# First attention of a two-layer Flamingo-style block on one Trainium2 core: router logits from the turned input rows, eight more output columns, and the two scatters of a tile set apart

## The chip, the cores and the metric

The kernel runs on one core of a Trainium2 chip. The metric is the device time of one launch in microseconds (us), the median of several runs. Five engines work side by side, each through its own list of instructions in order: TensorE (PE, with its weight loads as PEld), VectorE (DVE), ScalarE (ACT), GpSimd (POOL), and the queue engine SyncE (SP), which here only issues transfers. They wait for each other through semaphores.

## The reference

32 sequences of 128 rows and 256 columns (x), each with a context of the same size, go through two layers. Layer 0 is what the change touches:

```python
x = x + tanh(g_xattn[0]) * L0_xattn(layernorm(x), ctx, ctx)       # 16 heads of 16
# L0_ffn of layernorm(x), a mixture of 8 experts, the best 2 of each row:
xn = (x - mu) / sqrt(var + eps) * gamma + beta
logits = xn @ Wg.T + bg                                           # 8 columns
tp, ti = top_k(softmax(logits), 2)
x = x + tanh(g_ffn[0]) * (layernorm(x) + sum of the two experts' outputs, weighted)
```

Here the layernorm in front of the mixture and the one inside it fall together in the kernel. Layer 1 (an attention with a bias per key, then a soft mixture over 16 slots) is left as it is.

## The kernel before

The program is a row of stages: setup, attention 0 with routing, the mixture of layer 0 (`moe0`), attention 1, the slot mixture, the final attention. Each stage of attention 0 is written as a loop over steps k from -2 to B+3 (B = 32 tiles, one sequence each), written out in full; in step k several tiles are in flight, each at another point. No planner sets the order: on each engine it is the order of the lines in `tensor`, `scalar`, `vector`, `gpsimd` and `sync`.

In step k of attention 0 TensorE does, in this order (line numbers of the profile):

- `scores(k, 0)`: half of the scores of tile k (L575) and of the turned scores of tile k-1 (L584, L590); L674 turns the output of tile k-2 back into rows
- `keys(k+1)` (L611) and `values(k+1)` (L598, three products of rounded parts)
- L687: the rank of each row of tile k-4 among the rows of its experts
- L704 turns the normalised rows `xh` of tile k+1; L720 turns the rows `xn` of tile k-3, normalised after the attention, into `ps[4]`
- `scores(k, 1)`: the other half; L728 turns the attention result `att` of tile k-2
- L750: the queries of tile k+1 from `xT`; L757: the 8 logits of tile k-3 from `xnT`; L764: the output product of tile k-2
- L789 turns the row maxima, L802 multiplies scores by values.

ScalarE empties what this fills. Its order in a step is: L900 (`avS`), the exponentials of the first half (L903), the keys (four L838) and values (L848) of tile k+1, `xT` (L924), `xnT` (L937), `aT` (L947), the exponentials of the second half (L951), the queries (two L963), `mT` (L968). It waits for the values before it begins with the keys, and `xT` comes behind both.

VectorE takes the maxima of each half (L1023, L1090), normalises rows (L1061 writes `xn`, L1112 writes `xh`), picks the best two logits (L1116 to L1122), counts rows per expert (L1065 to L1081 give the row numbers `slot_i`), adds the output product to x (L1132), and scales x by the gated layernorm (L1073, L1075, L1137). GpSimd computes the inverse roots (L1210; L1169 and L1171), adds the output bias (L1223), splits the context into two rounded parts (L1186, L1188), in steps 8 to 23 a sixteenth of the first expert's weights as well (L1241), and at the end of a step issues the two indirect DMAs (L1251, a GpSimd instruction of its own each) that scatter the rows `xn` of tile k-4 to their experts' regions.

Which two scatters and when:

```python
pool.wait_ge(st_p.sem, st_p.at(k - 1, "b"))     # TensorE has issued both halves of the turned scores
pool.wait_ge(rk_v.sem, rk_v.at(k - 4, "put"))   # slot_i of the tile is there
for c in range(2):
    nc.gpsimd.indirect_dma_start(...)
```

Of the kernel before, what the change touches and what calls it, by code (L numbers as in the profile page):

```python
# [7 lines left out]
ALU = mybir.AluOpType  # L8
ACT = mybir.ActivationFunctionType
# [36 lines left out]
COLS = ["bq0", "bk0", "bv0", "dbq", "dbk", "cbq", "cbk", "cbv", "gamma", "beta"]  # L46
# [15 lines left out]
def build(nc, a, out):  # L62
    ctx = ExitStack()
    with ctx:
# [93 lines left out]
        xnT = carve(C, P)  # L158
# [142 lines left out]
        assert 2 * C * D + 2 * C * P <= 4 * 2 * D  # L301
        ctx_hi, ctx_lo = (rounded(f"ctx_{part}", spare_at + (2 + n) * C * P, C, P) for n, part in enumerate(("hi", "lo")))
# [66 lines left out]
        ld_late = sem("ld_late")  # L369
# [26 lines left out]
        xn_columns = xn.rearrange("p i d -> p (i d)")[:, 0:4 * P].rearrange("p (n t) -> p n t", n=4)  # L396

        def folded(pe):
            pe.wait_ge(setup_v, 4)
            pe.wait_ge(ld_const, 16 * 5)  # L400
            for c in range(C):
                nc.tensor.matmul(ps[7][:, 0:D], xn_columns[:, c, :], w["o0"][:, c, :], start=c == 0, stop=c == C - 1)
# [5 lines left out]
        def tables(dve):  # L408
# [7 lines left out]
            for c in range(C):  # L416
                nc.vector.tensor_scalar(xn_columns[:, C + c, :], ones[:, :], col["beta"][:, c:c + 1], None, ALU.mult)
                last = nc.vector.tensor_scalar(xn_columns[:, c, :], ones[:, :], col["bv0"][:, c:c + 1], None, ALU.mult)
# [6 lines left out]
        def folded_rows(dve):  # L425
            dve.wait_ge(setup_p, 1)
            nc.vector.tensor_tensor(row["bo0"], ps[7][:, 0:D], row["bo0"], ALU.add).then_inc(setup_v, 1)
            nc.vector.tensor_tensor(bg_sb[:, :], ps[7][:, D:D + E0], bg_sb[:, :], ALU.add).then_inc(setup_v, 1)
            for c in range(C):
                nc.vector.tensor_scalar(wg_sb[:, c, :], wg_sb[:, c, :], col["gamma"][:, c:c + 1], None, ALU.mult)  # L430
# [5 lines left out]
        def attention(L):  # L436
# [6 lines left out]
            pre_p = track(n + "pre_p", "xT Q")  # L443
# [12 lines left out]
            out_v = track(n + "out_v", "den att x")  # L456
            ln_g = track(n + "ln_g", "var rstd")
            if A:
                rt_p = track(n + "rt_p", "xnT lg")
                rk_p = track(n + "rk_p", "rank")  # L460
                rk_v = track(n + "rk_v", "oh both pos run ohp slot put")
                rt_a = track(n + "rt_a", "xnT")
                rt_v = track(n + "rt_v", "lg top idx keep")
                bias_g = track(n + "bias_g", "x")
                n2_v = track(n + "n2_v", "stats mean rv xn grow shift res")
                n2_g = track(n + "n2_g", "rstd")
# [36 lines left out]
            def sync(sp):  # L503
                for k in steps:
                    if A and k == B - 1:
                        sp.wait_ge(kv_p.sem, kv_p.at(B - 1, "V"))
                        sp.wait_ge(pre_p.sem, pre_p.at(B - 1, "Q"))
# [40 lines left out]
            def tensor(pe):  # L548
# [93 lines left out]
                if A:  # L642
                    pe.wait_ge(ld_first, 32)
# [17 lines left out]
                for k in steps:  # L661
# [6 lines left out]
                    if A and k == 2:  # L668
                        pe.wait_ge(setup_v, 6)
# [1584 lines left out]
```

## Time and profile before

| | |
|---|---|
| runs | 1352.38, 1355.66, 1358.79 us; median 1355.66 |
| the profiled execution | 1369.84 us, span 1368.0 us, mean granted TensorE clock 0.981 |
| attention 0 | about 6 to 350 us of the span; first product of `moe0` at 359.68 us |
| TensorE busy (share of the span) | 1297.2 us (95%) |
| VectorE / ScalarE / GpSimd busy | 930.5 / 794.5 / 712.2 us |

A step of attention 0 takes 9.5 to 9.8 us; the steps 8 to 23, with the expert weights on ScalarE and GpSimd, are the longer ones. Matmuls in fp32 stand as two records for each instruction. "Idle before" an instruction names the engine that released it; "issue" is idle time for which the profile shows no cause.

### The profile page before, as it was taken

How to read it: one execution, taken by the hardware profiler on the slowest of the kernel's cores; microseconds unless marked ns; L12 is line 12 of the kernel's file. 1: busy time of each engine (PE TensorE's matmuls, PEld its weight loads, DVE VectorE, ACT ScalarE, POOL GpSimd, SP SyncE). 2: the span in 40 equal slices, each digit the busy share in tenths (PEclk: the TensorE clock that was granted, in tenths of full speed). 3: DMA queues.
4: the chain of work that ended last, by engine and by line, in shares of the span. 5: the costliest groups of instructions: out<-in, count | busy, mean ns of one | idle time of the engine just before them, and what ended most of it. 6: DMA issues, size and time to landing. Idle time of an engine off the chain costs nothing.

```text
span 1368.0 us, 38200 instructions
## 1 busy us (share of the span) xinstructions
PE 1297.2 (95%) x14802; PEld 1154.4 (84%) x14802; DVE 930.5 (68%) x2484; ACT 794.5 (58%) x1761; POOL 712.2 (52%) x708
## 2 busy tenths in 40 slices
PE   6999999998889999999999998999999999899898
PEld 5888888886789999999999986889999998545476
DVE  4788888897576655556556216999999997412287
ACT  4566666663457777777777444666566665332454
POOL 1365656553266877778877024566665652200131
PEclk9999999999899999999999997999999999999999
DMA  6574545463457777776775921541121110499812
GB/s 196 186 246 157 182 146 182 148 202 98 158 178 215 221 227 225 232 227 220 221 224 190 375 80 33 174 164 48 53 60 48 49 41 17 172 429 432 355 56 70
DMA packets 103618, 237.24 MB, mean 173 GB/s; under 512 B 8976, under 2 KB 85904, under 8 KB 91024
## 3 DMA queue, kind: packets, MB, share of 16 engines
q1 hardware_dynamic: 97296, 218.02, 46.3%
q0 software_dynamic: 6144, 16.79, 3.9%
q8 instruction: 119, 1.95, 0.6%
q14 instruction: 59, 0.48, 0.1%
HBM read 173.96 MB, written 60.82 MB: 172 GB/s over the span
## 4 chain that ended last, share of the span: by engine, by line
PE 85%; DVE 8%; DMA 3%; issue 2%; ACT 2%; POOL 0%; SPq 0%; DVEq 0%; ACTq 0%; PEldq 0%; POOLq 0%
PE ps L1542 13%; PE psT L1527 7%; PE ps L598 5%; PE psS L575 5%; PE ps L802 5%; PE ps L750 4%; PE psT L584 4%; PE psS L1527 3%; PE ps L1527 3%; PE ps L611 3%; PE ps L735 2%; PE ps L764 2%; PE ps L674 2%; PE psT L590 2%; PE ps L1780 2%
## 5 line engine op out<-in xcount | busy, mean ns | idle before, releaser
L1495 POOL TENSOR_TENSOR wb_lo<-arena,wb_hi 128x2048 fp32r<-128x2048 f32 x64 | 298.0, 4657 | 104.4 <-ACT wb_hi L1615 104.4
L1542 PE MATMUL ps<-wb_hi,hT_hi 128*128 128x256 f32 x528 | 153.3, 290 | 6.5 <-DVE hT_lo L1668 6.5
L584 PE MATMUL psT<-arena 32*128 32x128 f32 x2048 | 155.3, 286 | 0.0
L1542 PE MATMUL ps<-wb_lo,hT_hi 128*128 128x256 f32 x528 | 148.6, 281 | 0.0
L1542 PE MATMUL ps<-wb_hi,hT_lo 128*128 128x256 f32 x528 | 148.6, 281 | 0.0
L575 PE MATMUL psS<-arena 32*128 32x256 f32 x1024 | 143.2, 397 | 0.7 <-ACT arena L963 0.7
L1615 ACT CAST wb_hi<-arena 128x1024 fp32r<-128x1024 f32 x128 | 130.6, 1044 | 6.5 <-DMA arena<-w_dram 6.2
L1169 POOL TENSOR_TENSOR arena<-arena,eps_sb 128x1 f32<-128x1 f32 x96 | 26.2, 273 | 203.2 <-DVE arena L1043 115.4
L584 PEld LDWEIGHTS psT<-arena 32*128 32x128 f32 x2048 | 129.2, 188 | 2.6 <-issue 1.8
L1680 DVE TENSOR_TENSOR arena<-ps,arena 128x512 f32<-128x512 f32 (+1 forms) x39 | 25.4, 650 | 120.1 <-PE ps L1542 79.7
L1542 PEld LDWEIGHTS ps<-wb_hi,hT_hi 128*128 128x128 f32 x528 | 100.3, 190 | 6.8 <-issue 6.7
L575 PEld LDWEIGHTS psS<-arena 32*128 32x128 f32 x1024 | 93.6, 189 | 13.6 <-issue 11.5
L1542 PEld LDWEIGHTS ps<-wb_lo,hT_hi 128*128 128x128 f32 x528 | 101.5, 192 | 0.0
L1177 POOL DMA_INDIRECT arena<-xs_rows,slot_i x64 | 64.3, 1005 | 69.3 <-DMA xs_rows<-arena 54.3
L1542 PEld LDWEIGHTS ps<-wb_hi,hT_lo 128*128 128x128 f32 x528 | 100.3, 190 | 0.0
L1090 DVE TENSOR_REDUCE arena<-psS 128x8 f32<-128x1024 f32 x64 | 78.1, 1220 | 24.3 <-PE psS L575 24.3
L1023 DVE TENSOR_REDUCE arena<-psS 128x8 f32<-128x1024 f32 x64 | 78.3, 1224 | 20.0 <-PE psS L575 18.7
L1630 ACT ACTIVATE psS<-psS,arena 128x256 f32<-128x256 f32 x66 | 26.8, 444 | 99.8 <-PE psS L1527 99.8
L1251 POOL DMA_INDIRECT xs_rows<-arena,slot_i x64 | 65.3, 1020 | 35.9 <-issue 15.5
L838 ACT ACTIVATE arena<-ps,bkm,const 128x128 f32<-128x128 f32 x128 | 48.1, 456 | 46.5 <-PE ps L598 34.4
L750 PE MATMUL ps<-arena,w_sb 128*128 128x128 f32 x512 | 71.0, 283 | 2.8 <-ACT arena L924 2.8
L802 PE MATMUL ps<-arena 128*32 128x128 f32 x2048 | 70.0, 277 | 0.2
(385 smaller groups left out, 3894.4 us busy)
## 6 DMA issues: line engine op xcount, KB each, us to landing
arena<-wset_dram SPq DMA_DIRECT2D x24, 2048.0 KB, 15.5
xs_rows<-arena SPq DMA_DIRECT2D x33, 1024.0 KB, 8.2
arena<-w_dram SPq DMA_DIRECT2D x32, 1028.0 KB, 6.0
arena<-w_dram SPq DMA_DIRECT2D x32, 1024.0 KB, 5.9
arena<-w_dram SPq DMA_DIRECT2D x7, 2052.0 KB, 12.9
w_sb<-xs_rows SPq DMA_DIRECT2D x33, 256.0 KB, 2.7
xs_rows<-arena SPq DMA_DIRECT2D x33, 256.0 KB, 5.5
arena<-ctxT_dram SPq DMA_DIRECT2D x63, 128.0 KB, 2.4
```

What stands on the lines that cost most here:

```text
L575: last = nc.tensor.matmul(psS[:, b, c * D:(c + 1) * D], qT[p, k % 3, c, :], kbd[p, k % 3, c, :, :], start=A, stop=A or c == 1, skip_group_ ...
L584: nc.tensor.matmul(psT[:, b, j * P:(j + 1) * P], kbd[p, (k - 1) % 3, c, par, :], qT[p, (k - 1) % 3, c, :], start=j == 0, stop=False, skip_ ...
L598: last = nc.tensor.matmul(out_, left[i_][:, c, :], right[j_][:, c, :], start=n_ == 0 and c == 0, stop=n_ == 2 and c == C - 1)
L750: last = nc.tensor.matmul(ps[6][:, m * P:(m + 1) * P], wq[:, c, m * P:(m + 1) * P], xT[:, c, :], start=c == 0, stop=c == C - 1)
L802: last = nc.tensor.matmul(ps[4][32 * j:32 * (j + 1), g * P:(g + 1) * P], vz[:, (k - 1) % 3, 4 * g + j, :, :], pT[:, g, j * P:(j + 1) * P], ...
L1023: nc.vector.tensor_reduce(mx[:, 0:2, :], psS.rearrange("p b (j t) -> p b j t", j=4), AX, ALU.max, negate=True).then_inc(mx_v.sem, 1)
L1090: nc.vector.tensor_reduce(mx[:, 2:4, :], psS.rearrange("p b (j t) -> p b j t", j=4), AX, ALU.max, negate=True).then_inc(mx_v.sem, 1)
L1251: nc.gpsimd.indirect_dma_start(out=xs_dram[:, :], out_offset=bass.IndirectOffsetOnAxis(ap=slot_i[:, c, k - 4:k - 3].bitcast(U32), axis=0), ...
L1495: nc.gpsimd.tensor_tensor(wb_lo[:, u % 2, part], wb_raw[:, u % 2, part], wb_hi[:, u % 2, part], ALU.subtract).then_inc(w_g.sem, 1)
L1527: last = nc.tensor.matmul(ps[1 + f // 2][:, o:o + 2 * P], wp[:, c, f * P:(f + 1) * P], xp[:, c, :], start=n == 0 and c == 0, stop=n == 2 a ...
L1542: last = nc.tensor.matmul(ps[5][:, t * D:(t + 1) * D], hp[:, f, t * P:(t + 1) * P], wp[:, f, :], start=f == 0 and t == 0 and n == 0, stop= ...
L1615: last = nc.scalar.copy(wb_hi[:, b, o:o + F0], wb_raw[:, b, o:o + F0])
```

## The change

The logits no longer need the rows after the attention turned on TensorE. With x the input rows, a the attention's output before its output matrix Wo, t = tanh(g), and W the router's columns times gamma with their mean taken out, the sum (x + t (a Wo + bo) ) W is x W + t a (Wo W) + t bo W, and the layernorm's factor is applied to it afterwards. So:

- `wc` (W) is made in the setup by VectorE, with a product of ones on TensorE for the mean (`gate_sums`); Wo W takes four small products with a turned copy of Wo that is loaded in addition (`gate_through_output`) and stands behind Wo as 8 more columns of `wo_wide`; the bias row takes four more (`gate_biases`).
- TensorE: L720 is gone; the logits' product takes `xT` of tile k+1 and `wc`, right behind the queries; the output product has 264 columns for 256.
- ScalarE: `xnT` (L937) is gone; in its place it scales x by the gated layernorm (before VectorE's L1137); behind `mT` comes a small activation that undoes the input's normalisation on the 8 logit columns (`u`).
- VectorE: L1073, L1075 and L1137 are gone; one small operation comes in (`lg_sum`).
- GpSimd: four small operations come in (`spread`, `grow`, `shift`, `u`); the bias is added a step later; the second scatter of a tile is issued a step later, behind the first half of the scores, and the first one before the context parts.

The diff, cut to its core:

```diff
+        def gate_sums(pe):
+            pe.wait_ge(fold_v, 1)
+            for c in range(C):
+                last = nc.tensor.matmul(ps[4][:, 0:E0], ones[:, :], wc[:, c, :], start=c == 0, stop=c == C - 1)
...
+        def gate_through_output(pe):
+            pe.wait_ge(fold_v, 3)
+            for m in range(C):
+                for c in range(C):
+                    last = nc.tensor.matmul(ps[7][:, D + (1 + m) * E0:D + (2 + m) * E0], wo_turned[:, c, m * P:(m + 1) * P],
+                                            wc[:, c, :], start=c == 0, stop=c == C - 1)
...
+        def gate_biases(pe):
+            pe.wait_ge(fold_v, 4)
+            pe.wait_ge(setup_v, 6)
...
                 if A:
-                    pe.wait_ge(ld_first, 32)
+                    gate_sums(pe)
+                    pe.wait_ge(ld_first, 48)
                     pe.wait_ge(ld_kv, 16)
...
-                    if A and valid(k - 3):
-                        pe.wait_ge(n2_v.sem, n2_v.at(k - 3, "xn"))
...
-                        for c in range(C):
-                            last = nc.tensor.transpose(ps[4][:, c * P:(c + 1) * P], xn[:, (k - 3) % 3, c * P:(c + 1) * P],
-                                                       cv["ident"])
...
-                    if A and valid(k - 3):
-                        pe.wait_ge(rt_a.sem, rt_a.at(k - 3, "xnT"))
+                    if A and valid(k + 1):
...
-                            last = nc.tensor.matmul(ps[5][:, D:D + E0], xnT[:, c, :], wg_sb[:, c, :],
-                                                    start=c == 0, stop=c == C - 1)
+                            last = nc.tensor.matmul(ps[5][:, D:D + E0], xT[:, c, :], wc[:, c, :], start=c == 0, stop=c == C - 1)
...
-                                last = nc.tensor.matmul(ps[7][:, D:2 * D], aT[:, c, :], wo[:, c, :],
+                                last = nc.tensor.matmul(ps[7][:, 0:D + E0], aT[:, c, :], wo_wide[:, c, :],
...
                     if A and valid(k - 3):
-                        act.wait_ge(rt_p.sem, rt_p.at(k - 3, "xnT"))
-                        nc.scalar.copy(xnT.rearrange("p c t -> p (c t)"), ps[4][:, 0:D]).then_inc(rt_a.sem, 1)
+                        act.wait_ge(n2_g.sem, n2_g.at(k - 3, "shift"))
+                        act.wait_ge(n2_v.sem, n2_v.at(k - 3, "xn"))
+                        nc.scalar.activation(x_all[:, k - 2], x_all[:, k - 2], ACT.Identity, bias=rs[:, 1:2], scale=rs[:, 0:1])\
+                            .then_inc(n2_a.sem, 1)
...
-                    if A and valid(ln_i):
-                        dve.wait_ge(n2_v.sem, n2_v.at(ln_i, "shift"))
-                        nc.vector.tensor_scalar(x_all[:, ln_i + 1], x_all[:, ln_i + 1], rs[:, 0:1], rs[:, 1:2],
-                                                ALU.mult, ALU.subtract).then_inc(n2_v.sem, 1)
...
+                    if A and valid(k - 5):
+                        if valid(k - 1):
+                            pool.wait_ge(st_p.sem, st_p.at(k - 1, "a"))
+                        scatter(k - 5, 1)
```

**TensorE, a whole step between the values of tile k+1 and the maxima.** Before, from the row of values on (the numbers are lines of the kernel before):

```order
L598 MATMUL ps<-v_hi,ctx_lo 128x256 x2
L687 MATMUL ps<-both_r,before_r 128x8
L687 MATMUL ps<-both_r,both_rows 128x8
L704 MATMUL ps<-const,arena 128x128 x2
L720 MATMUL ps<-const,arena 128x128 x2
L575 MATMUL psS<-arena 128x256 x2
```

The rows from the second half's end on, before:

```order
L728 MATMUL ps<-const,arena 128x128 x2
L750 MATMUL ps<-arena,w_sb 128x128 x4
L757 MATMUL ps<-wg_sb,arena 128x8 x2
L764 MATMUL ps<-w_sb,arena 128x256 x2
L789 MATMUL ps<-ident_b,m_49 128x128
```

The same two places with the change (L648 is the old L598, L740 the old L687, L757 the old L704, L625 the old L575, L795 the old L750, L802 the logits, L808 the output):

```order
L648 MATMUL ps<-v_hi,ctx_lo 128x256 x2
L740 MATMUL ps<-both_r,before_r 128x8
L740 MATMUL ps<-both_r,both_rows 128x8
L757 MATMUL ps<-const,arena 128x128 x2
L625 MATMUL psS<-arena 128x256 x2
```

```order
L773 MATMUL ps<-const,arena 128x128 x2
L795 MATMUL ps<-arena,w_sb 128x128 x4
L802 MATMUL ps<-arena 128x8 x2
L808 MATMUL ps<-arena 128x264 x2
L833 MATMUL ps<-ident_b,m_49 128x128
```

Two instructions (L720) are gone between the values and the queries; behind the queries the count is the same.

**GpSimd, one step with a piece of the expert weights.** Before, from the row of the inverse roots on:

```order
L1210 TENSOR_TENSOR arena<-arena,mhalf 128x2 [waits a0_n2_v]
L1169 TENSOR_TENSOR arena<-arena,eps_sb 128x1 [waits a0_ln_v]
L1171 TENSOR_TENSOR arena<-arena,mhalf 128x1 [waits a0_ln_g]
L1223 TENSOR_TENSOR x_all<-x_all,row_sb 128x256 [waits a0_ln_v]
L1186 TENSOR_SCALAR ctx_hi<-arena 128x256 [waits a0_kv_p,a0_ld_ctx1]
L1188 TENSOR_TENSOR ctx_lo<-arena,ctx_hi 128x256 [waits rest_g]
L1241 TENSOR_TENSOR wb_lo<-arena,wb_hi 128x256 [waits first_hi]
L1251 DMA xs_rows<-arena,slot_i 33792x256 [waits a0_rk_v,a0_st_p,zeroed1]
L1251 DMA xs_rows<-arena,slot_i 33792x256
```

With the change (L1261 is a scatter, L1292 and L1293 are `grow` and `shift`, L1234 is `spread`, L1311 is `u`):

```order
L1284 TENSOR_TENSOR arena<-arena,mhalf 128x2 [waits a0_n2_g,a0_rt_v,a0_n2_v]
L1261 DMA xs_rows<-arena,slot_i 33792x256 [waits a0_st_p]
L1292 TENSOR_SCALAR arena<-arena,tg 128x1 [waits a0_n2_a,a0_n2_g]
L1293 TENSOR_SCALAR arena<-arena 128x1
L1228 TENSOR_TENSOR arena<-arena,eps_sb 128x1 [waits a0_ln_g,a0_ln_v]
L1230 TENSOR_TENSOR arena<-arena,mhalf 128x1 [waits a0_ln_g]
L1234 TENSOR_TENSOR arena<-arena 128x1 [waits a0_u_a,a0_ln_g]
L1307 TENSOR_TENSOR x_all<-x_all,row_sb 128x256 [waits a0_ln_v]
L1311 TENSOR_TENSOR arena<-arena 128x8 [waits a0_u_a]
L1261 DMA xs_rows<-arena,slot_i 33792x256 [waits a0_rk_v,a0_st_p,zeroed1]
L1250 TENSOR_SCALAR ctx_hi<-arena 128x256 [waits a0_kv_p,a0_ld_ctx1]
L1252 TENSOR_TENSOR ctx_lo<-arena,ctx_hi 128x256 [waits rest_g]
```

One scatter now stands second in the step, ahead of `grow` and `shift`, which ScalarE waits for; the other stands ahead of the context parts.

## Rows read from the trace of the kernel before

**Rows 1.** windows, 103:260: length, busy PE, PEld, DVE, ACT, POOL

```profile
103.00:260.00 157.00, 154.91 (x2248) 135.06 (x2247) 137.76 (x501) 100.81 (x239) 96.15 (x143) 1.00 0.49 165
```

**Rows 2.** waits of the weight loads, 58:316, then twice 316:349: us, times, longest

```profile
PEld ps L720 <- DVE arena L1061: 5.6, 15, 0.4
...
PEld ps L720 <- DVE arena L1061: 4.7, 4, 1.6
...
PEld ps L757 <- ACT arena L937: 1.2, 2, 0.7
```

**Rows 3.** timeline, step 19: start, us, engine, line

```profile
203.48 0.48 PE L598 MATMUL ps<-v_hi,ctx_hi 128*128 128x256 f32 x2
...
204.47 1.50 ACT L838 ACTIVATE arena<-ps,bkm,const 128x128 f32<-128x128 f32 x4 [1.17 <-PE ps L598]
...
204.94 0.20 PEld L720 LDWEIGHTS ps<-const,arena 128*128 128x128 f32 x2 [0.33 <-DVE arena L1061]
...
205.31 0.19 PEld L575 LDWEIGHTS psS<-arena 32*128 32x128 f32 x2 [0.17 <-issue]
...
206.11 0.40 ACT L924 COPY arena<-ps 128x256 f32<-128x256 f32 x1
...
206.92 1.06 PE L750 MATMUL ps<-arena,w_sb 128*128 128x128 f32 x8
```

**Rows 4.** timeline, step 26

```profile
271.32 0.48 PE L598 MATMUL ps<-v_hi,ctx_hi 128*128 128x256 f32 x2
...
273.95 0.41 ACT L924 COPY arena<-ps 128x256 f32<-128x256 f32 x1
...
274.82 1.06 PE L750 MATMUL ps<-arena,w_sb 128*128 128x128 f32 x8
...
278.22 0.48 PE L575 MATMUL psS<-arena 32*128 32x256 f32 x2
```

**Rows 5.** timeline, step 2 (no L720, no L687)

```profile
34.91 0.47 PE L598 MATMUL ps<-v_hi,ctx_hi 128*128 128x256 f32 x2
...
37.53 0.40 ACT L924 COPY arena<-ps 128x256 f32<-128x256 f32 x1
...
37.99 1.16 PE L750 MATMUL ps<-arena,w_sb 128*128 128x128 f32 x8 [0.21 <-ACT arena L924]
```

**Rows 6.** groups by line, 60 to 316 us: busy us, mean ns, idle before

```profile
L1090 DVE TENSOR_REDUCE arena<-psS 128x8 f32<-128x1024 f32 x27 | 33.1, 1225 | 14.6 <-PE psS L575 14.6
...
L1112 DVE TENSOR_SCALAR arena<-x_all,arena 128x256 f32<-128x256 f32 x26 | 13.0, 501 | 0.0
...
L1137 DVE TENSOR_SCALAR x_all<-x_all,arena 128x256 f32<-128x256 f32 x27 | 11.2, 413 | 0.0
...
L1251 POOL DMA_INDIRECT xs_rows<-arena,slot_i x54 | 55.4, 1026 | 18.0 <-issue 14.0 <-PE psT L590 4.0
...
L1169 POOL TENSOR_TENSOR arena<-arena,eps_sb 128x1 f32<-128x1 f32 x25 | 7.0, 281 | 43.4 <-DVE arena L1057 43.4
```

**Rows 7.** timeline, PE, step 3

```profile
43.74 0.48 PE L598 MATMUL ps<-v_hi,ctx_hi 128*128 128x256 f32 x2
...
46.45 0.44 PE L720 MATMUL ps<-const,arena 128*128 128x128 f32 x2 [1.52 <-DVE arena L1061]
...
48.62 1.92 PE L750 MATMUL ps<-arena,w_sb 128*128 128x128 f32 x8
...
55.00 0.48 PE L575 MATMUL psS<-arena 32*128 32x256 f32 x2
```

**Rows 8.** windows, 48 to 50 us; 0.53 is the granted clock

```profile
48.00:50.00 2.00, 2.00 (x17) 1.90 (x12) 1.86 (x6) 1.14 (x2) 0.84 (x2) 0.53 1.06 369
```

**Rows 9.** timeline of TensorE, setup

```profile
6.44 2.07 PE L611 MATMUL ps<-arena,w_sb 128*128 128x128 f32 x8 [6.44 <-DMA col_sb<-cols_dram]
...
22.86 0.51 PE L404 MATMUL ps<-wg_sb,arena 128*128 128x8 f32 x4
```

**Rows 10.** timeline of TensorE, last rank matmul of stage one

```profile
348.13 0.54 PE L687 MATMUL ps<-both_r,before_r 128*128 128x8 f32 x1
```

More of the change, by code:

```diff
@@ L157, in build @@
         xn = carve(3, D)
-        xnT = carve(C, P)
+        small_at = place[0]
+        wc = carve(C, E0)
+        lg_x = carve(4, E0)
+        lg_row = carve(E0)
+        lg_sum = carve(E0)
+        spread = carve(4)
+        ntg = carve(1)
+        carve(C * P - (place[0] - small_at))
         xc = carve(D)
@@ L666, in tensor @@
                         queries(pe, 0, 6)
+                    if A and k == 2:
+                        gate_biases(pe)
                     scores(k, 0)
                     if A and k == 2:
-                        pe.wait_ge(setup_v, 6)
+                        pe.wait_ge(fold_v, 5)
                     if valid(k - 2):
@@ L795, in tensor @@
                         if A:
-                            before(pe, rt_a.sem, rt_a.at(k - 3, "xnT"))
                             before(pe, rk_v.sem, rk_v.at(k - 4, "run") if valid(k - 4) else 0)
@@ L807, in tensor @@
                         folded(pe)
+                        gate_through_output(pe)
                     if A and k == B + 2:
@@ L968, in scalar @@
                         nc.scalar.copy(mT[:, :], ps[6][:, 0:P]).then_inc(m_a.sem, 1)
+                    if A and valid(k + 1):
+                        act.wait_ge(pre_p.sem, pre_p.at(k + 1, "x"))
+                        act.wait_ge(ln_g.sem, ln_g.at(k + 1, "spread"))
+                        before(act, out_v.sem, out_v.at(k - 3, "t"))
+                        nc.scalar.activation(lg_x[:, (k + 1) % 4, :], ps[5][:, D:D + E0], ACT.Identity, bias=0.0,
+                                             scale=spread[:, (k + 1) % 4:(k + 1) % 4 + 1]).then_inc(u_a.sem, 1)
                     if not A and valid(k - 4):
@@ L1007, in vector @@
                         dve.wait_ge(n2_v.sem, n2_v.at(ln_i, "stats"))
+                        before(dve, n2_g.sem, n2_g.at(ln_i - 1, "shift"))
                         nc.vector.bn_aggr(mv[:, 1, :], stat[:, 1, :]).then_inc(n2_v.sem, 1)
@@ L2148, in vector @@
                                         cv["parity"][:, None, :].to_broadcast([P, C, 2]), ALU.mult).then_inc(setup_v, 1)
+                for c in range(C):
+                    last = nc.vector.tensor_scalar(wc[:, c, :], wg_sb[:, c, :], col["gamma"][:, c:c + 1], None, ALU.mult)
+                last.then_inc(fold_v, 1)
             return sync, None, None, vector, None
```

174 lines of the change are left out of this document (116 added, 58 removed).

## The prediction

> **What bounds the kernel now.** I read the windows view first. In the long middle of attention 0, TensorE is busy for 154.91 of 157 us, VectorE for 137.76, ScalarE for 100.81, GpSimd for 96.15 [rows 1]. A step there takes some 9.7 us, so TensorE's list in order is the bound, VectorE is next with 8.5 us a step, and the other two have 3 us to spare. Then I asked what TensorE's weight loads wait for: between 58 and 316 us only L720, for VectorE's `xn`, 5.6 us in total [rows 2]. So L720 costs its wait and its own slot. The reader should see that the time of one step is a closed walk through TensorE's list, and that one piece of this walk has a second limit beside it. In step 19 the first product of the values starts at 203.48, the queries (L750) at 206.92: 3.44 us. In this stretch ScalarE waits for the values (L838, idle 1.17 us until TensorE's L598), does the keys, the value copy and `xT` (L924, from 206.11 for 0.40 us, to 206.51), and only then may L750 start [rows 3]. In step 26 the same is 271.32 to 274.82, 3.50 us, with L924 done at 274.36 [rows 4].
>
> **Steady steps.** The change takes L720 out of this stretch and adds nothing to it. On TensorE alone this is the wait of 0.33 and the load of 0.20, after which L575 would come at 204.78 where it is at 205.31: 0.53 us earlier [rows 3]. But ScalarE's chain starts at the values and doesn't move. Step 2 shows the stretch without L720 (and without L687): values at 34.91, L924 done at 37.93, L750 at 37.99 after waiting for L924; 3.08 us, of which 0.06 lies between L924's end and L750 [rows 5]. So L750 can't come before 206.51 + 0.06 = 206.57 in step 19 (gain 0.35) and 274.42 in step 26 (gain 0.40). The other 0.13 to 0.18 us become a new wait, of L750 for ScalarE. From L750 on, TensorE's list is as long as before: the logits' product only moves ahead of other data, and the output has 8 more columns in 256, which by L404's size (4 records of 8 columns, 0.51 us, [rows 9]) is bounded by 0 and some 0.25; I take 0.03, since the output's own time is by columns. In steps 4 to 30 queries and L720 both occur: 16 with the expert weights, 16 x 0.32 = 5.1 us; 11 without, 11 x 0.37 = 4.1. Together **-9.2 us**; bounds: 0, if another engine takes the place of L720's wait, and 27 x 0.53 = 14.3.
>
> What hides the rest. VectorE loses L1137 (413 ns on average) and two of about 0.2 to 0.3, and gains one of some 0.15 on 8 columns. In its second half it still sits idle 14.6 us over 27 steps before L1090, 0.54 each [rows 6]; the scores come 0.53 earlier and VectorE is ready earlier by the two small ones, so some 0.2 to 0.3 us of that idle time stay. The scaling of x moves to ScalarE in the place of a copy of the same size, and a small one comes behind `mT`; ScalarE has 3 us a step. Behind the waiting scaling stand `aT`, the second exponentials and the queries' copies, and for them L764 and L802; so `shift` must not be late. GpSimd needs for it L1210's result, one scatter (1026 ns and some 0.26 of issue gap) and two operations of 281 ns [rows 6]: about 2.6 us after L1210 starts, where ScalarE comes to it some 4.7 us after (L924's end at 206.51 [rows 3]). GpSimd's whole step grows from 96.15/157 of 9.7 = 5.9 us busy by 4 x 0.28 = 1.1 to 7.1, plus issue gaps. The transfers themselves are 2 scatters of a tile as before, through the same queue; `xn`'s buffer is used again three tiles later, so a scatter issued a step later still has a step to land.
>
> The Trainium skill speaks against this place for a scatter. L1112 and the same operation elsewhere differ by what runs beside them: L1112, beside the scatters, takes 501 ns, L1137 takes 413 [rows 6]. The Trainium skill, SBUF — State Buffer, section "SBUF: two separate sides", says that VectorE in some modes and GpSimd lock each other out of one shared pair of ports for a whole instruction. By the row this is 0.1 us on one operation; by that rule a scatter could hold one VectorE operation for its whole 1.0 us, in a part of the step where VectorE has only some 0.25 us of idle time left, which is the second rival.
>
> **Step 3.** Here L720 waits 1.52 us, the queries come 4.88 us after the values (43.74 to 48.62), and TensorE then runs at half its clock (granted 0.53 [rows 8], so 1.2 GHz for most of it): L750 takes 1.92 us instead of 1.06, and from L750 to the next step's L575 at 55.00 are 6.38 us, against 3.40 in step 26 [rows 4, 7]. With ScalarE's chain as the limit the queries come at 43.74 + 3.08 = 46.8: **-1.8**. If TensorE then keeps 2.4 GHz, another 6.38 - 3.40 = **-3.0**. The idle stretch of 1.52 us stands just before the fall, and shrinks to a few tenths; but whether the fall hangs on it no row shows. I take it as the likelier, bounds 0 and 3.0.
>
> **Setup.** TensorE's first product waits for a load (6.44 [rows 9]) and then runs without a break. Now `gate_sums` comes first: it waits for one more load in the list and VectorE's two scalings of it, and is two products of 8 columns: 0.5 by L404, plus some 0.9 for the wait, between 0.5 and 2: **+1.4**. `gate_through_output` and `gate_biases` are four such products each, on TensorE's path: **+1.8**. The logits' product begins four steps earlier; in steps -1 to 1 it lies in a wait for the queries' copy, in step 2 it doesn't: **+0.4**. On GpSimd the first bias, which waited for the setup, moves out of the way of the first context parts: -0.1. Sum **+3.5** (2 to 6).
>
> **The end of the stage.** In steps 31 to 34 there are no keys, so L720's waits are bare: 4.7 us in 4 times, and L757 waits 1.2 for `xnT` [rows 2]. Those 5.9, four loads of 0.2 and four logits' products of 0.5 make 8.7 us that leave TensorE's list; the lower bound is 0. VectorE's and ScalarE's chains give part back: in step 31, the second maxima can come only 1.2 earlier, and steps 32 and 33 are bound by exponentials and `aT`, so little comes there. The last rank matmul (348.13 [rows 10]) stands behind the ahead-of-time products of attention 1 in TensorE's list, and two waits and four instructions leave the list just before it. I take **-3.6**, from 1.2 in step 31, 0.7 by step 33, 1.7 in step 34, nearer the lower end. The routing and `moe0`'s first product come behind it by the same amount.
>
> **Sum.** -9.2 - 1.8 - 3.0 + 3.5 - 3.6 = -14.1 us. The profiled execution, 1369.84 us (span 1368.0 and 1.8 around it), would become 1355.7. It lies 14.2 above the median of the runs shown, 1355.66; taken off this median the forecast is **1341.5 us**. Without the clock's 3.0 it is 1344.5.
>
> **Rivals.** (1) *Only the setup and the tail change.* Another chain closes the steady step at its old length: VectorE, whose remaining idle time the fuller GpSimd beside it eats up. Then -1.8 + 3.5 - 3.6 = -1.9, or with the clock -4.9: 1351 to 1354. For it: GpSimd is fuller, and L1112 shows that the two touch each other. Against: L1090's idle time is real now, and three VectorE operations leave. Chance 0.14. (2) *Slower: `shift` comes too late.* GpSimd's scatter stands ahead of `grow` and `shift`, ScalarE waits for them with `aT` and the exponentials behind it. It decides if the scatter, measured at 1.0, takes over 1.0 + 2.1 = 3.1 us; each microsecond beyond costs 27 to 32 us. At 4 us this is 0.8 x 30 = 24 - 4.9 = +19: 1375. The rule of the ports would be its cause. Against: 54 scatters average 1026 ns, though VectorE works through all of them. Chance 0.07. (3) *The forecast without the clock*, or with other falls of it instead: part of the forecast's own range. (4) *More than forecast*, the tail at its upper bound, 8.7: 1336.
>
> **How the numbers follow.** Forecast with its variants (3) and (4): 0.79. A measurement of this kernel tells about 0.5% (6.8 us) from no change. Faster by more, below 1348.9: 0.78; within: 0.14; slower: 0.08. The range takes in the upper bound of the tail and the lower edge of rival 1: 1334 to 1352.
>
> **What would show it.** L750 must wait for ScalarE's L924 in nearly every step, 0.1 to 0.2 us, and the steps must take 9.1 us without and 9.4 with the expert weights. L808 (the output) must not wait for `aT`. Step 3 must take some 9.7 us at full clock instead of 13.9. TensorE's first keys should start at about 7.8 us. The last rank matmul should come some 14 us earlier than 348.13. Wrong would be: L750 without a wait, ScalarE waiting for GpSimd's `shift`, or L1090 without idle time in front of it.

## The result

The changed kernel took 1349.53 us (median of 20 runs, 1341.31 to 1357.38), the kernel before 1363.57 beside it (20 runs, 1351.39 to 1368.82). The estimate of the ratio from all runs is 0.9925, 95% interval 0.9903 to 0.9947: 0.75%, or 10.2 us, faster. The means of the runs lie 11.1 us apart (1350.43 and 1361.55) and the medians 14.0; this text goes by the estimate that has an interval. A second series of 12 runs (after_again) gives 0.9915 (0.9883 to 0.9947). The profiled execution took 1357.0 us with a span of 1355.2, against 1369.84 and 1368.0 before.

The windows of the changed kernel over the middle of attention 0 answer to [rows 1]:

```profile
core 0: us, PE busy (x) PEld busy (x) DVE busy (x) ACT busy (x) POOL busy (x), PEclk, DMA share, GB/s
103.00:260.00 157.00, 156.19 (x2321) 135.32 (x2321) 145.86 (x491) 110.02 (x270) 120.56 (x220) 1.00 0.53 176
```

VectorE is fuller (145.86 of 157 where it was 137.76), although work left it. The waits of TensorE's weight loads from 58 to 307 us answer to [rows 2] (us in total, times, longest):

```profile
PEld psS L625 <- issue: 9.7, 53, 0.2
PEld ps L795 <- ACT arena L972: 7.0, 27, 0.3
PEld ps L833 <- issue: 4.5, 25, 0.2
PEld ps L845 <- issue: 1.5, 7, 0.3
PEld ps L648 <- POOL ctx_lo L1252: 0.8, 1, 0.8
```

The reader is to see that L720's wait is gone and that the queries (L795, before L750) wait for ScalarE's `xT` (L972, before L924) in each of 27 steps, 0.26 us each. In the timeline of a step, answering to [rows 3], TensorE's and ScalarE's rows that matter are:

```profile
209.87 0.48 PE L648 MATMUL ps<-v_hi,ctx_hi 128*128 128x256 f32 x2
210.87 1.50 ACT L882 ACTIVATE arena<-ps,bkm,const 128x128 f32<-128x128 f32 x4 [1.18 <-PE ps L648]
212.26 0.38 ACT L892 COPY arena<-ps 128x256 f32<-128x256 f32 x1
212.51 0.40 ACT L972 COPY arena<-ps 128x256 f32<-128x256 f32 x1
212.77 0.64 ACT L986 ACTIVATE x_all<-x_all,arena 128x256 f32<-128x256 f32 x1
212.96 0.97 PEld L795 LDWEIGHTS ps<-arena,w_sb 128*128 128x128 f32 x8 [0.26 <-ACT arena L972]
212.96 1.16 PE L795 MATMUL ps<-arena,w_sb 128*128 128x128 f32 x8
213.28 0.40 ACT L997 COPY arena<-ps 128x256 f32<-128x256 f32 x1
213.53 1.07 ACT L1001 ACTIVATE arena<-psT 128x1024 f32<-128x1024 f32 x1
214.32 1.14 PE L808 MATMUL ps<-arena 128*128 128x264 f32 x4
214.44 0.67 ACT L1013 ACTIVATE arena<-ps,qcol 128x128 f32<-128x128 f32 x2
215.30 0.22 PE L833 MATMUL ps<-ident_b,m 128*128 128x128 bf16 x1
```

Values to queries are 3.09 us (209.87 to 212.96); the step is 9.26 to 9.27 long in most cases. Between the first products of the values in step 2 and in step 30 lie 260.95 us, 259.90 in the second profile; before they were 274.58, and 271.02 in a second profile of the old kernel.

The early part costs more than it did, and runs partly at half clock (1.2 GHz):

```profile
10.00:20.00 10.00, 8.39 (x58) 6.57 (x57) 6.41 (x24) 4.91 (x15) 1.55 (x5) 1.00 0.73 254
20.00:30.00 10.00, 9.54 (x64) 8.82 (x63) 2.42 (x6) 2.89 (x8) 0.54 (x2) 0.54 0.27 93
30.00:40.00 10.00, 8.96 (x124) 7.64 (x124) 3.91 (x13) 4.60 (x12) 2.75 (x5) 0.84 0.40 134
```

Step 2's values start at 41.90, 7.0 later than in the old profile [rows 5], which has half clock itself from 14.0 to 17.4 us.

### The profile page after: what moved, and what is told of

Read it like the earlier page. It is cut to its first block, busy times and chain, and to the rows that moved or that the text cites. A ratio compares the mean times of both kernels' runs of the same rounds, so it can differ in the third digit from the quotient of the medians.

```text
span 1355.2 us, 38313 instructions
## 1 busy us (share of the span) xinstructions
PE 1287.3 (95%) x14758; PEld 1145.5 (85%) x14758; DVE 932.6 (69%) x2426; ACT 805.6 (59%) x1794; POOL 748.0 (55%) x836
## 4 chain that ended last, share of the span: by engine, by line
PE 83%; DVE 6%; DMA 4%; issue 2%; ACT 2%; POOL 1%; SPq 1%; DVEq 0%; ACTq 0%; POOLq 0%; PEldq 0%
PE ps L1632 12%; PE psT L1617 6%; PE ps L648 6%; PE psS L625 5%; PE ps L795 5%; PE ps L845 5%; PE psT L634 4%; PE ps L661 4%; PE ps L1617 3%; PE psS L1617 3%; PE ps L780 2%; PE ps L727 2%; PE ps L808 2%; PE psT L640 2%; DMA arena<-w_dram 2%
## 5 line engine op out<-in xcount | busy, mean ns | idle before, releaser
L634 PE MATMUL psT<-arena 32*128 32x128 f32 x2048 | 151.9, 287 | 0.4 <-ACT arena L948 0.4
L625 PE MATMUL psS<-arena 32*128 32x256 f32 x1024 | 143.5, 399 | 1.2 <-ACT arena L948 0.5
L1705 ACT CAST wb_hi<-arena 128x1024 fp32r<-128x1024 f32 x128 | 130.6, 1045 | 13.4 <-DMA arena<-w_dram 13.2
L625 PEld LDWEIGHTS psS<-arena 32*128 32x128 f32 x1024 | 95.4, 191 | 13.6 <-issue 10.6
L1147 DVE TENSOR_REDUCE arena<-psS 128x8 f32<-128x1024 f32 x64 | 78.0, 1219 | 11.1 <-PE psS L625 10.8
L1261 POOL DMA_INDIRECT xs_rows<-arena,slot_i x64 | 68.7, 1073 | 19.7 <-issue 11.5
L795 PE MATMUL ps<-arena,w_sb 128*128 128x128 f32 x512 | 72.8, 286 | 3.1 <-ACT arena L972 2.6
L795 PEld LDWEIGHTS ps<-arena,w_sb 128*128 128x128 f32 x512 | 63.4, 195 | 12.0 <-ACT arena L972 10.8
## 6 DMA issues: line engine op xcount, KB each, us to landing
arena<-wset_dram SPq DMA_DIRECT2D x24, 2048.0 KB, 14.6
arena<-w_dram SPq DMA_DIRECT2D x7, 2052.0 KB, 13.6
```

What stands on the lines that cost most here:

```text
L625: last = nc.tensor.matmul(psS[:, b, c * D:(c + 1) * D], qT[p, k % 3, c, :], kbd[p, k % 3, c, :, :], start=A, stop=A or c == 1, skip_group_ ...
L634: nc.tensor.matmul(psT[:, b, j * P:(j + 1) * P], kbd[p, (k - 1) % 3, c, par, :], qT[p, (k - 1) % 3, c, :], start=j == 0, stop=False, skip_ ...
L795: last = nc.tensor.matmul(ps[6][:, m * P:(m + 1) * P], wq[:, c, m * P:(m + 1) * P], xT[:, c, :], start=c == 0, stop=c == C - 1)
L1147: nc.vector.tensor_reduce(mx[:, 2:4, :], psS.rearrange("p b (j t) -> p b j t", j=4), AX, ALU.max, negate=True).then_inc(mx_v.sem, 1)
L1261: nc.gpsimd.indirect_dma_start(out=xs_dram[:, :], out_offset=bass.IndirectOffsetOnAxis(ap=slot_i[:, c, i:i + 1].bitcast(U32), axis=0), in_ ...
L1705: last = nc.scalar.copy(wb_hi[:, b, o:o + F0], wb_raw[:, b, o:o + F0])
```

## The experiments

"Step" below is the time between the first products of the values of two tiles (L598 or L648), median of the profile; "ring steps" are the 16 with the expert weights. All ratios are to the kernel before, run beside it in the same series. The edits are cut to their core.

**The two kernels again.** after_again:

> The changed kernel itself once more, for a second ratio and a second profile. Theory S (the clock's falls hang on where TensorE's work stands): half clock again at about 21 to 31 and 38 to 41.5 us, the scores of step 3 at 48 +- 1 us, span about 1355. Theory R (the falls wander from run to run): half clock in other stretches, the scores of step 3 at 44.5 to 45.5 us, because plain products add only 3.5 us to the 41.1 of the kernel before; mean granted clock and time then move together, about 1.2 us for each 0.001. Both: ratio between 0.990 and 0.995, steady steps 9.26 to 9.37 us.

Theory R held: half clock fell in other places (granted clock 0.83 from 30 to 40 us, 1.00 from 20 to 30), the scores of step 3 came at 45.06, and the span was 1345.7. Steps 4 to 30 take 9.25 to 9.41, median 9.27. before_again:

> The kernel before once more, for a second profile. Theory R (the falls of the clock wander between executions): no half clock in step 3 (48 to 55 us), the stretch from the values of step 3 to those of step 4 takes 9.9 to 10.9 us instead of 13.89 (4.88 or less from values to queries), and the first values of the steady steps (step 2) come at 33 to 34.9 us. Theory S (the fall hangs on the wait of 1.52 us in step 3): half clock again at 48 to 55 us, 13.9 us for this step.

Windows of before_again:

```profile
20.00:27.00 7.00, 7.00 (x50) 6.34 (x50) 1.74 (x3) 1.95 (x4) 0.74 (x2) 0.51 0.27 89
48.00:55.00 7.00, 7.00 (x122) 6.22 (x123) 5.41 (x19) 3.68 (x8) 2.66 (x5) 1.00 1.02 324
```

The kernel before has its half clock at 20 to 27 us here, and none at 48 to 55, though L720's wait in step 3 is even longer (1.77 us where it was 1.52); that step takes 10.71 us instead of 13.89. Step 2's values came at 36.01, not at 33 to 34.9, since a longer fall now lies ahead of them. So the fall in step 3 was no property of the kernel, and the wait alone doesn't bring it. Over the changed kernel's 20 runs, mean granted clock and time go together (correlation -0.85, 1.2 us for each 0.001): runs at 0.978 to 0.981 took 1353.4 to 1357.0 us, those at 0.989 and 0.990 took 1341.3 to 1347.5. The runs tell more than the profiles here: the mean granted clock averages 0.9838 over 32 runs of the changed kernel (both series) and 0.9810 over the 31 runs of the kernel before in the second series. A straight line through each group of runs gives 1351.0 and 1358.0 us at one clock, 0.983: 7.0 us between the kernels at the same clock, and some 3.3 more (0.0028 at 1.2 us for each 0.001) that go with the higher clock.

**One move alone.** turn_late, made from the kernel before:

```
@@ def tensor: the block of L720 (wait for xn, transposes into ps[4])
-   ... ahead of scores(k, 1)
+   ... behind the turning of att (L728), right ahead of the queries (L750)
```

> The kernel before with one move: TensorE's turning of xn (L720) stands right ahead of the queries instead of ahead of the second scores; routing, output and setup stay as before. Theory M (what the change saves in a steady step is the wait of L720 of 0.33 us, and ScalarE's chain allows no more): values to queries falls from 3.43 to 3.50 to about 3.1 us, 27 steps give 8 to 9 us, step 3 gives 1.5, the tail 1 to 3, and nothing is paid in the setup: ratio about 0.991. Rival L (the move makes xnT late on ScalarE, with aT, the exponentials and L764 behind it): a wait of 0.2 to 0.4 us appears at L757 or L764 in each step, ratio 0.997 to 1.0.

Ratio 0.9917 (0.9877 to 0.9958), span 1343.7. Values to queries 3.13, steps 9.45 with and without the expert weights. This one move gives as much as the whole change. The steps gave less than theory M had said, though: from the values of step 4 to those of step 30 are 245.7 us, against 251.9 and 251.5 in the two profiles of before, 6 us and not 8 to 9. What closes its step is not the queries: the mT product (L788, before L789) waits.

```profile
PEld ps L788 <- DVE m L1099: 5.4, 15, 0.4
PEld ps L788 <- issue: 3.6, 10, 0.4
```

The view names VectorE's `m` or nothing. `m` was ready 4.60 us after the values, in the ring steps 5.14; mT's product started at 5.56 in both; the queries' copies on ScalarE (L962) ended at 5.42. mT's product is written into the bank that these copies read, and waits for them.

**What closes it.** turn_late_scaled: turn_late and, from the change, the scaling on ScalarE (here behind the copy of `mT`), `grow` and `shift` on GpSimd, and the scatters apart.

```
@@ def vector
-   rs[:, 0:1], rs[:, 1:2] (L1073, L1075); scaling of x_all (L1137)
@@ def scalar, behind the copy of mT
+   nc.scalar.activation(x_all[:, k - 2], ..., bias=rs[:, 1:2], scale=rs[:, 0:1]).then_inc(n2_a.sem, 1)
@@ def gpsimd
+   scatter(k - 5, 1) and rs[:, 0:1], rs[:, 1:2] behind rq; scatter(k - 4, 0) ahead of context_parts(k + 2)
```

> The kernel before with xn turned ahead of the queries (as in turn_late), and two parts of the change alone: the scaling of x on ScalarE with its two small operations on GpSimd, and the scatters of a tile apart. Logits, output and setup as before. Theory (turn_late's 9.44 us are VectorE's: mT's product waits 0.35 us for its m; without the scaling and the two small operations VectorE does 0.9 us less and TensorE's list closes the step at 3.1 + 6.05 to 6.17): steps 9.2 to 9.25 us, no wait for m, nothing paid in the setup, ratio 0.985 to 0.988 to the kernel before, 5 to 8 us less than the changed kernel. Rival (ScalarE or GpSimd becomes late instead): steps 9.4 to 9.5, ratio 0.992.

Ratio 0.9891 (0.9849 to 0.9934), span 1343.3, steps 9.44. My theory fell: VectorE now had 0.5 us of idle time ahead of each of its two maxima (8.3 and 6.9 us in 15 steps each), `m` was ready at 4.76, and the step was no shorter: mT's product still started at 5.56, 0.14 after the end of the queries' copies. scale_on_vector, the changed kernel with one operation moved back:

```
@@ def scalar / def vector
-   nc.scalar.activation(x_all[:, k - 2], ..., bias=rs[:, 1:2], scale=rs[:, 0:1]).then_inc(n2_a.sem, 1)
+   nc.vector.tensor_scalar(x_all[:, ln_i + 1], x_all[:, ln_i + 1], rs[:, 0:1], rs[:, 1:2], ALU.mult, ALU.add)
```

> The changed kernel with the scaling of x (L986 on ScalarE, 0.64 us) back on VectorE behind the output's addition, where it took 0.41. Theory M (the removal of L720 alone made the step shorter; VectorE has room): steps stay at 9.27 us. Rival V (the change's steady gain needs VectorE's relief as well): mT's product waits for m by 0.1 to 0.3 us, steps 9.4 to 9.55 us, 4 to 7 us in all.

Neither: steps 9.21 to 9.22, shorter by 0.05, with VectorE busy for 138.96 of 147 us (one execution, 1343.35 us). So VectorE doesn't close the changed step, and the scaling is better off on VectorE. Without it on ScalarE the queries' copies end at 4.92 instead of 5.24, and mT's product starts at 5.43 all the same; TensorE now waits 0.27 us before L845 in 24 steps, which the view puts down to "issue".

**ScalarE's order.** xt_first:

```
@@ def scalar
+   copy of xT (L972) ahead of keys(k + 1, 6), values(k + 1, 6)
@@ def tensor
-   queries into ps[6]          # keys and values are read from bank 6
+   queries into ps[5]
```

> The changed kernel with ScalarE's copy of the turned input rows (xT) ahead of the keys' and values' copies, and the queries' products in bank 5, so that they need not wait until ScalarE has read the keys and values out of bank 6. Theory M (after the change the step is closed by ScalarE's chain from the values to xT): the wait of the queries' product for xT, 7.0 us in 27 steps, is gone, values to queries falls from 3.08 to about 2.85, steps 9.05 to 9.12 us, and the kernel is 6 to 7 us shorter than the changed one: ratio to the kernel before about 0.988. Rival V (VectorE, 9.3 us less 0.7 idle in a step, closes it right behind): TensorE's wait reappears at L833 or at the scores, steps stay at 9.2 to 9.3 us, ratio 0.992.

Ratio 1.0026 (0.9992 to 1.0059), steps 9.68: slower than the changed kernel by 0.4 us a step. Values to queries did fall, to 2.91. But `xT` is ready on TensorE only after the values, so ScalarE waits 1.58 us and starts the keys at 1.69 us after the values instead of 1.00; its queries' copies end at 5.65 instead of 5.24, and mT's product, for which I had left the wait on them, starts at 5.80 instead of 5.43:

```profile
PE ps L834 <- ACT arena L1021: 5.6, 15, 0.4
```

xt_second repairs both:

```
@@ def scalar:  keys(k + 1, 6); copy of xT; values(k + 1, 6)
@@ def tensor, ahead of mT's product
-   before(pe, pre_a.sem, pre_a.at(k + 1, "Q"))
+   pe.wait_ge(kv_a.sem, kv_a.at(k + 1, "V"))      # queries in ps[5]
```

> The changed kernel with ScalarE's list in the order keys, xT, values (it was keys, values, xT), the queries' products in bank 5, and the mT product waiting for the values' copy alone instead of for the queries' copy. Theory M (ScalarE's chain from the values to xT closes the changed step, and nothing else stands right behind it): the wait of L795 for xT is gone, values to queries falls from 3.09 to about 2.87, no wait takes its place, steps 9.05 to 9.1 us, 27 steps give 5 to 6 us against the changed kernel, ratio 0.987 to 0.989. Rival V (VectorE closes the step right behind): the mT product waits for VectorE's m by 0.1 to 0.25 us and the steps stay at 9.2 to 9.27, ratio 0.992.

Ratio 0.9816 (0.977 to 0.9862), median 1335.95 of 6 runs, span 1333.5: better than both kernels, and by more than theory M had said. Its step:

```profile
216.05 0.48 PE L649 MATMUL ps<-v_hi,ctx_hi 128*128 128x256 f32 x2
218.43 0.38 ACT L966 COPY arena<-ps 128x256 f32<-128x256 f32 x1
218.68 0.40 ACT L896 COPY arena<-ps 128x256 f32<-128x256 f32 x1
218.86 0.97 PEld L796 LDWEIGHTS ps<-arena,w_sb 128*128 128x128 f32 x8
218.96 1.07 PE L796 MATMUL ps<-arena,w_sb 128*128 128x128 f32 x8
220.22 1.14 PE L809 MATMUL ps<-arena 128*128 128x264 f32 x4
220.62 0.67 ACT L1021 ACTIVATE arena<-ps,qcol 128x128 f32<-128x128 f32 x2
221.20 0.22 PE L837 MATMUL ps<-ident_b,m 128*128 128x128 bf16 x1
```

The queries wait for nothing, and mT's product starts while the queries' copies (L1021, 220.62 to 221.29) still run. The step is 8.94 to 8.95, nearly all of it TensorE's own list; what is left is 0.2 to 0.3 us before L849 in 16 steps ("issue", 3.7 us) or before mT's product for `m` in 10 (2.9 us), rival V's wait, which cost nothing that the steps show. One more thing shows: without a wait the first weight load (218.86) lies 0.10 ahead of its product (218.96), under the one before; behind a wait, load and product start together (both 212.96 above), and the group takes 1.16 instead of 1.07. From queries to output (L809) are 1.26 us, with the wait 1.36. q_wait_kept puts the one wait back:

> xt_second with one thing put back: the mT product waits for the queries' copy on ScalarE again. Theory (ScalarE's chain meets TensorE's list twice in a step, at the queries and again at mT's product, which starts 0.19 us after the queries' copies end): mT starts 5.43 us after the values instead of 5.15, steps 9.2 to 9.25 us; the new order of ScalarE's list alone gives almost nothing. Rival (one meeting point, at the queries): the steps stay at 8.95 us.

Steps 9.26 to 9.27, mT's product 5.38 after the values, 0.15 after the end of the copies: the theory held. The new order of ScalarE's list and the other bank give next to nothing (9.27 to 9.26) as long as mT's product waits for the queries' copies. The other half, the shorter wait without the new order, was not run.

**The scatters.** scatters_together, made from the changed kernel:

```
@@ def gpsimd
-   scatter(k - 5, 1)      # behind rq (L1284)
-   scatter(k - 4, 0)      # ahead of context_parts(k + 2)
+   scatter(k - 4, 0); scatter(k - 4, 1)      # at the end of the step
```

> The changed kernel with both scatters of a tile back at the end of the step, together; all else as changed. Theory N (where they stand is worth nothing, since nobody waits for GpSimd): steps 9.26 to 9.37 us as before, ratio 0.991 to 0.994 against the kernel before, but single VectorE operations that lay beside a scatter (L1169 614 ns, L1173 442 ns, L1180 401 ns) fall back toward 500, 153 and 185 ns and others slow down instead. Rival P (a scatter slows VectorE where the step is nearly bound by it): the steps become 0.1 us shorter or longer, 3 us in all.

Ratio 0.9927 (0.9893 to 0.996), span 1345.7. Steps 9.27 without the expert weights, 9.50 with them: rival P in its ring steps, 16 x 0.23 = 3.7 us. Not the scatter makes `m` late here, but what stands before it. A ring step of it, VectorE, GpSimd and mT's load:

```profile
209.97 0.73 POOL L1252 TENSOR_TENSOR ctx_lo<-arena,ctx_hi 128x256 fp32r<-128x256 f32 x1
210.00 0.73 DVE L1151 CAST m<-arena 128x16 bf16<-128x16 f32 x1
210.66 0.73 POOL L1328 TENSOR_TENSOR wb_lo<-arena,wb_hi 128x256 fp32r<-128x256 f32 x1
210.76 0.66 DVE L1153 TENSOR_TENSOR arena<-arena,m 128x16 f32<-128x16 f32 x1
211.55 1.08 POOL L1261 DMA_INDIRECT xs_rows<-arena,slot_i  x1 [0.16 <-issue]
211.66 0.17 DVE L1157 TENSOR_TENSOR m<-arena,m 128x16 bf16<-128x16 f32 x1
211.89 0.10 PEld L833 LDWEIGHTS ps<-ident_b,m 128*128 128x128 bf16 x1 [0.47 <-DVE m L1157]
```

Two VectorE operations on 16 columns, 0.17 us elsewhere, last 0.73 and 0.66: until GpSimd's operation on 256 columns beside them ends. L1157, which starts 0.11 us after the scatter, takes its plain 0.17. That one row doesn't clear the scatter. In the changed kernel itself L1155 here starts 0.33 us after a scatter and lasts until the scatter's end:

```profile
167.31 1.09 POOL L1261 DMA_INDIRECT xs_rows<-arena,slot_i  x1 [0.17 <-issue]
167.43 0.18 DVE L1153 TENSOR_TENSOR arena<-arena,m 128x16 f32<-128x16 f32 x1
167.64 0.73 DVE L1155 CAST m<-arena 128x16 bf16<-128x16 f32 x1
```

L1155 takes 0.61 to 0.73 us in 9 of 26 steps of this profile and 0.17 in most others; `m` is ready in time even so. no_scatters was to settle this:

```
@@ def gpsimd of turn_late
-   both indirect_dma_start (L1251 of the kernel before), and the waits on their semaphores
```

> turn_late without the 64 scatters of attention 0 (the sorted rows are never written, the experts work on what the buffer holds). Theory H (a scatter holds the VectorE operation that lies beside it, 0.4 to 0.5 us each): L1093 falls from 687 to about 175 ns, L1080 from 613 to 170, L1136 from 528 to 410, VectorE is busy 0.9 to 1.1 us a step less, the wait of mT's product for m (0.35) is gone, steps 9.1 to 9.2 us. Rival F (VectorE is simply full, the scatters only shift who is late): VectorE's busy time falls by under 0.2 us and the steps stay at 9.4.

Median step 9.44, L1092 still 0.72 us in the ring steps and L1079 0.61: there theory H fell. For two operations on 256 columns it held. With the scatters (turn_late) and without them (no_scatters):

```profile
L1136 DVE TENSOR_SCALAR x_all<-x_all,arena 128x256 f32<-128x256 f32 x26 | 12.8, 491 | 0.0
L1111 DVE TENSOR_SCALAR arena<-x_all,arena 128x256 f32<-128x256 f32 x25 | 11.9, 476 | 0.0
```

```profile
L1110 DVE TENSOR_SCALAR arena<-x_all,arena 128x256 f32<-128x256 f32 x25 | 10.2, 407 | 0.0
L1135 DVE TENSOR_SCALAR x_all<-x_all,arena 128x256 f32<-128x256 f32 x25 | 10.1, 405 | 0.0
```

So a scatter costs each of these 0.07 to 0.09 us on average (0.54 and 0.60 us where they are held), and VectorE is busy for 137.91 instead of 139.55 of 147 us: 0.1 us a step, of the size that rival F had named. But the bound that rival F named, VectorE, was wrong too (turn_late_scaled). The rows of the two that stayed long, beside GpSimd's wide operations:

```profile
203.68 0.72 POOL L1221 TENSOR_TENSOR x_all<-x_all,row_sb 128x256 f32<-128x256 f32 x1
203.81 0.62 DVE L1079 CAST slot_i<-slot_f 128x2 int32<-128x2 f32 x1
205.55 0.72 POOL L1239 TENSOR_TENSOR wb_lo<-arena,wb_hi 128x256 fp32r<-128x256 f32 x1
205.59 0.72 DVE L1092 CAST m<-arena 128x16 bf16<-128x16 f32 x1
```

before_split, the kernel before with the scatters apart and nothing else:

```
@@ def gpsimd
-   for c in range(2): nc.gpsimd.indirect_dma_start(...)      # at the end of the step
+   scatter(k - 5, 1)      # behind rq (L1210)
+   scatter(k - 4, 0)      # ahead of context_parts(k + 2)
```

> The kernel before with only the scatters of a tile apart, placed as in the changed kernel. Theory N (GpSimd isn't waited for before the change, and VectorE's m is ready 0.5 us ahead of need): steps 9.53 to 9.57 us without the expert weights and 9.7 to 9.75 with them, as before; no part of the gain. Rival P (the two scatters behind each other are what costs the steps with the expert weights 0.2 us): all steps 9.5 to 9.55, 3 to 4 us less.

Span 1355.0. Rival P: nearly all steps 9.53 to 9.64, where the ring steps had 9.7 to 9.9. In the kernel before, the first scores of a ring step take 0.24 us longer than elsewhere (from their start to L674 1.57 instead of 1.33): the fourfold groups of L575 start 0.32, 0.54 and 0.84 us after the first in place of 0.32, 0.54 and 0.75, with no wait for an engine in the view. This stall is gone with the scatters apart, and in turn_late as well, which keeps them together. What holds TensorE there no run shows.

## Why the prediction was right or wrong

**The forecast of 1341.5 us was 8 too low**, though the sign, the range and the place of the gain held. Two steps of it failed, and they are about the level and the clock, not about the repeating step. "If TensorE then keeps 2.4 GHz, another -3.0. I take it as the likelier": a fall of the clock in one profile was booked as a property of the kernel. before_again has none there, after a wait of 1.77 us, and takes 10.71 us for the step. The second: "taken off this median". 1355.66 was the median of three runs, where 20 runs (these three among them) give 1363.57 and 31 others 1359.69: the level was 4 to 8 us too low. The runs of one kernel spread over 16 to 21 us, and for the changed kernel most of that goes with the granted clock. Without the 3.0 the working gives -11.1 us, 0.8%, which lies in the intervals of both measured ratios (0.75% and 0.85%). The runs do show some 3 us that go with a higher clock of the changed kernel, but they are not those of step 3.

**Steady steps, -9.2: right in the sum (-9.5 in the profiles of the two kernels and -10.3 in their second ones, from the scores of step 4 to those of step 31), half by luck.** The limit was where I put it: 3.08 to 3.11 from values to queries in every step, with a new wait for L972. Its size was 0.26, not 0.13 to 0.18, and it costs 0.10 more, for the weight load that no longer lies under a product; so a step without the expert weights gained 0.29 (9.56 to 9.27) instead of 0.37. "TensorE's list is as long as before" from the queries on was the mis-sized term. In the ring steps 0.46 were gained where I had 0.32: the stall of 0.24 in the first scores, which I hadn't seen, went with the scatters, a part of the change to which I gave no gain (before_split: ring steps 9.73 to 9.56; scatters_together: 9.27 to 9.50 when they are put back). So the steps are 9.27 of either kind, where I had named 9.1 and 9.4. What I missed altogether is that ScalarE meets TensorE a second time, at mT's product. I had read L720 as the only wait between 58 and 316 us; the same answer has mT's product (L789) in every one of the 27 steps, with no cause named:

```profile
PEld ps L789 <- issue: 4.3, 27, 0.2
PEld ps L720 <- issue: 4.0, 12, 0.3
```

(L720's own wait was 9.6 us by this, not 5.6.) Where the queries' copies do hold mT's product (turn_late, xt_first, q_wait_kept) it starts 0.14 to 0.15 us after their end. In the changed kernel it starts 0.19 after it (5.24 and 5.43), and at 5.43 also in scale_on_vector, where the copies end at 4.92. So TensorE's own list arrives at 5.43, and the copies would hold it from 5.29 on: 0.05 us are between the two, which is why moving the queries alone gave next to nothing.

**VectorE (rival 1)**: not the bound of the step, as forecast, but its idle time shrank for the reason that the rival gave. L1147 (before L1090) is preceded by 3.1 us of idle time in 27 steps, where it was 14.6 [rows 6], since operations beside GpSimd's are held, beside its wide ones above all. **`shift` (rival 2)**: no step waited for it, and the scatters took 1.08 us on average where it was 1.03. (At 4 us for a scatter the working should have had 0.9 x 30 and 1378, not 0.8 and 1375.) The doubt about the scatter's place had ground but too small a reach. L1112's 501 against 413 ns [rows 6] is the scatter's doing, as taken: in that profile L1112 has nothing but scatters beside it, takes 0.41 to 0.61 us, and without the scatters 0.41 in every step (no_scatters, L1110). L1137 was no clean counterpart, for it lies beside a scatter too, in 17 of 25 steps, mostly at its very end. What I hadn't seen is that GpSimd's work on 256 columns holds VectorE more: L1169, the same operation as L1112, takes 614 ns in the changed kernel.

**Step 3, -1.8**: 10.71 at full clock in before_again and 9.22 in after_again, -1.5. **Setup, +3.5**: right at full clock. Step 2's values start at 33.25, 33.68, 33.36 and 32.35 us in four kernels with the old setup (before_split, turn_late, turn_late_scaled, no_scatters) and at 36.83, 36.89, 36.22 and 35.18 in four with the new one (scatters_together, scale_on_vector, xt_second, xt_first), all without a fall of the clock by then: 33.2 and 36.3 on average, 3.1 us. The keys started at 7.86 (forecast 7.8). In the profiled execution the setup cost 7.0, the rest being half clock (13.6 us of it ahead of these values, against 3.4 before).

**The end of the stage, -3.6: about right at full clock, and more in the profiles.** From the values of step 30 to the first product of the experts were 52.04 and 53.60 us in the two profiles of before, and 46.10 and 44.97 in the two of after: 5.9 to 8.6 less. But this stretch has falls of the clock too, and most in the old kernel (granted clock in the last column but two, first before and before_again, then after and after_again):

```profile
309.49:361.50 52.01, 41.77 (x423) 35.31 (x421) 31.68 (x148) 17.06 (x36) 16.24 (x19) 0.90 0.31 100
307.03:360.60 53.57, 43.86 (x423) 36.56 (x421) 31.38 (x148) 17.16 (x36) 16.24 (x19) 0.84 0.31 98
302.85:348.90 46.05, 36.45 (x397) 30.58 (x395) 33.01 (x139) 17.97 (x37) 22.60 (x36) 0.93 0.33 104
298.38:343.30 44.92, 35.32 (x397) 29.69 (x395) 32.71 (x138) 17.87 (x37) 22.38 (x35) 0.96 0.34 106
```

By these shares 10.2 and 17.1 us of the stretch ran at half clock before, 6.8 and 3.4 with the change. If half clock costs half its length (in step 3 of before it was 3.2 us for 6.9), the stretch would be 46.9 and 45.1 us at full clock before, 42.7 and 43.3 with the change: an estimate of 1.8 to 4.2 less, 3.0 in the middle. So the profiles don't show the bound of 8.7. Why the old kernel has more half clock here no run shows. The last rank matmul came at 337.39, 10.7 us earlier than [rows 10], where I had said 14; the setup's half clock alone is 3.9. turn_late has 47.71 for the stretch, 44.3 at full clock, so over half of it is the bare wait of L720.

What stays open: the terms at full clock add up to 3.1 - 1.5 - 9.9 - 3.0 = -11.3 us. The runs give -7.0 at one and the same clock and -10.2 (-7.2 to -13.2) as they came. Stages that no edit touches differ by up to 8 us between profiles (998.45 to 1006.47 from the experts' first product to the end), so two profiles of each kernel can't settle these 4 us. The changed kernel got the higher clock on average (0.9838 against 0.9810); in the profiles it had more of it at the end of the stage, but which of the edits brings that no run shows.

## What to carry to other kernels

When a wait leaves one engine's list, walk the step once more through the engine that fed the next instruction, and name every place where the lists meet, also those that only a shared bank makes and that the view calls "issue": here the new order and bank gave nothing until the second wait was shortened too, and then 0.32 us a step, about what the change itself had saved in a step. Read a term from the step that repeats, never from one fall of the clock; take out the half clock before two stretches are compared, by the granted clock of each, and try the cheapest single move first: turning `xn` later in TensorE's list, right ahead of the queries, gave as much as the whole change with no setup to pay. Take the level from as many runs as the spread asks for, not from three.

## What the chip showed that I had not expected

GpSimd's elementwise operations on two inputs of 256 columns (0.72 to 0.73 us) hold a VectorE operation that starts beside them until they end: 0.62 to 0.75 us where 0.17 is plain (L1079, L1092, L1151, L1153). VectorE's maxima (L1147, read from PSUM) keep their 1.22 us beside the same operations. A scatter of 1.08 us holds less: in all twelve profiles with scatters, an operation that starts in its first 0.25 us takes its plain time (L1157 0.17, at most 0.06 more), while casts, TENSOR_SCALAR and TENSOR_TENSOR that start 0.3 to 0.7 us into it are often held to its end (L1155 up to 0.73 us for 0.17, L1112 up to 0.61 for 0.41). MAX8, the row statistics and what reads PSUM kept their time beside scatters too. The Trainium skill, SBUF — State Buffer, section "SBUF: two separate sides", states such a lock between the two engines for a whole instruction. The rows agree for GpSimd's elementwise work; for the scatter they agree for its later part alone, where I had weighed it as a whole.

TensorE's clock falls to half (1.2 GHz) at places that change from execution to execution of one kernel. In the first 60 us these were 14 to 17.4 and 48 to 55 us in one profile of the old kernel, 20 to 27 in the other; 21 to 31 and 38 to 41.5 us in one of the new, 34.4 to 37.8 in the other. In the steady steps between 60 and 310 us none of the thirteen profiles has a fall.
